# Moving the second half of a 32x32-tiled recurrence off the array's diagonal, with its residual masked by VectorE

## What is computed

```python
k = rope(x @ Wk.T); v = x @ Wv.T          # (B, H, S, 32), B = 4, H = 16
def step(W, kv):                          # W starts as the identity, 32 x 32 for each of 64 (batch, head)
    kc, vc = kv                           # 16 tokens
    z = einsum('bhsd,bhde->bhse', kc, W)
    grad = einsum('bhsd,bhse->bhde', kc, (z - vc) * inv_n)
    return (W - LR * grad, z)
_, zs = lax.scan(step, W0, (k_c, v_c))    # 32 steps
out = layernorm(zs) * ln_gamma + ln_beta; attn = out @ Wo.T
x = layernorm(x + attn)
```

## Time and profile before

| | us |
|---|---|
| median of 3 runs (lowest, highest) | 699.45 (698.92, 700.35) |
| the profiled execution's own time | 699.14 |
| its span in the profile | 697.3 |
| PE busy in the span | 677.9 (97%) |
| DVE busy | 443.7 (64%) |
| ACT busy | 315.0 (45%) |
| POOL busy | 305.8 (44%) |

### The profile page before, as it was taken

How to read it: one execution, slowest core, us unless ns; L and a number is a source line. 1 busy time by engine, 2 the same in 40 slices (tenths; PEclk the granted TensorE clock), 3 DMA queues, 4 the chain that set the end, 5 groups by cost and what they waited for, 6 DMA issues and landing times.

```text
span 697.3 us, 16575 instructions
## 1 busy us (share of the span) xinstructions
PE 677.9 (97%) x6884; PEld 547.4 (78%) x6884; DVE 443.7 (64%) x772; ACT 315.0 (45%) x599; POOL 305.8 (44%) x342
## 2 busy tenths in 40 slices
PE   9999999999999999999999999999999999999994
PEld 7767777777877778787888788888887888888883
DVE  4998676778856455378875554645466357666565
ACT  5653544545645532341123465655576452141232
POOL 2657667767636532011004345434552235626232
PEclk9999999999999999999999999999999999999998
DMA  8221242331341424000062577677547765414222
GB/s 277 87 65 46 66 141 66 93 111 52 110 154 64 141 61 156 31 14 1 1 241 78 195 273 256 208 273 259 179 161 253 260 204 182 121 60 123 74 76 90
DMA packets 65710, 92.47 MB, mean 133 GB/s; under 512 B 16672, under 2 KB 31776, under 8 KB 65632
## 3 DMA queue, kind: packets, MB, share of 16 engines
q1 hardware_dynamic: 59952, 72.76, 30.9%
q0 software_dynamic: 5680, 18.62, 9.2%
HBM read 67.56 MB, written 23.79 MB: 131 GB/s over the span
## 4 chain that ended last, share of the span: by engine, by line
PE 65%; DVE 17%; issue 5%; POOL 5%; ACT 4%; DMA 2%; DVEq 0%; POOLq 0%; ACTq 0%
PE bank L1255 13%; PE bank L1168 10%; PE bank L1061 10%; PE bank L1292 7%; PE bank L1115 6%; PE bank L1181 4%; PE bank L1094 4%; PE bank L1081 3%; DVE x L1465 3%; PE bank L1242 2%; DMA xg<-yd,SI 2%; DVE x L1513 2%; PE bank L1268 2%; POOL xg L1832 2%; DVE sg L1455 2%
## 5 line engine op out<-in xcount | busy, mean ns | idle before, releaser
L1794 POOL TENSOR_TENSOR xl<-RAW,xh 128x1024 fp32r<-128x1024 f32 x23 | 55.4, 2409 | 124.9 <-ACT xh L1655 124.8
L1168 PE MATMUL bank<-XH,GH 128*128 128x512 f32 x256 | 101.7, 397 | 0.5 <-ACT sg L1669 0.3
L1671 ACT ACTIVATE ah<-sg 128x512 fp32r<-128x512 f32 x48 | 30.3, 632 | 158.0 <-DVE sg L1455 158.0
L1168 PE MATMUL bank<-XH,GL 128*128 128x512 f32 x256 | 99.8, 390 | 0.0
L1168 PE MATMUL bank<-XL,GH 128*128 128x512 f32 x256 | 99.7, 390 | 0.0
L1455 DVE TENSOR_TENSOR sg<-sg,bank 128x512 f32<-128x512 f32 x48 | 32.9, 685 | 78.5 <-PE bank L1255 42.3
L1807 POOL DMA_INDIRECT xg<-x1d,idxu x39 | 42.3, 1085 | 69.9 <-DVE idxu L880 41.2
L1445 DVE TENSOR_TENSOR GL<-RAW,GH 128x1024 fp32r<-128x1024 f32 x42 | 50.3, 1224 | 11.0 <-ACT GH L1650 8.5
L1168 PEld LDWEIGHTS bank<-XH,GH 128*128 128x128 f32 x256 | 48.1, 188 | 11.3 <-ACT sg L1669 0.7
L1457 DVE TENSOR_TENSOR al<-sg,ah 128x512 fp32r<-128x512 f32 x48 | 35.2, 734 | 33.5 <-ACT ah L1671 32.8
L1168 PEld LDWEIGHTS bank<-XH,GL 128*128 128x128 f32 x256 | 48.1, 188 | 10.3
(11 more groups left out here) (254 smaller groups left out, 1608.9 us busy)
## 6 DMA issues: line engine op xcount, KB each, us to landing
RAW<-in_wgu SPq DMA_DIRECT2D x13, 1024.0 KB
yd<-RAW SPq DMA_DIRECT2D x39, 256.0 KB
RAW<-in_wsgu SPq DMA_DIRECT2D x14, 512.0 KB
RAW<-in_wd SPq DMA_DIRECT2D x13, 512.0 KB, 5.5
x<-in_xtok SPq DMA_DIRECT2D x16, 256.0 KB, 3.0
x1d<-x SPq DMA_DIRECT2D x16, 256.0 KB, 2.5
RAW<-in_wsd SPq DMA_DIRECT2D x8, 512.0 KB, 4.0
out_x<-x SPq DMA_DIRECT2D x16, 256.0 KB, 2.0
```

The lines of the kernel that those rows point to most:

```text
L1168: t = e.matmul(bank[b][:], (GL if wl else GH)[:, w % 2, k, c:c + 128], (XL if xlo else XH)[q % 2][:, k, :], start=(k == 0 and not wl and n ...
L1794: e.tensor_tensor(DL[:, w % 2, :, :], draw[:, raw_of(w), :, :], DH[:, w % 2, :, :].bitcast(F32), ALU.subtract).then_inc(*mark("low p", "d" ...
```

## The change

The second half (h = 1) moves to tiles off the diagonal: in z it takes rows g and columns (g + 64) % 128, in g rows (g + 64) % 128 and columns g. Its residual, values and rows of z thereby lie 64 partitions away from where they were, and so the host swaps the matching rows of Wv, Wo, gamma and beta. Within a block the two halves now alternate: four matmuls of half 0, four of half 1, for each `pp`. A block waits for both halves' operands before it begins.

The mask of half 1 goes from ScalarE to VectorE: one TENSOR_TENSOR with the mask behind the two subtractions (`rmask v`), where ScalarE had two ACTIVATEs. The mask of half 0 stays. The key turn for u >= 4 becomes two STREAM_TRANSPOSEs of 64 partitions that cross over, where there was one of 128.

```diff
                     for pp in range(4):
-                        hg, bp = 2 * h + pp // 2, pp % 2
-                        c = hg * 512 + (n % 8) * 64 + bp * 32
-                        for g in range(0, 128, 32):
-                            t = e.matmul(bank[h][g:g + 32, pp * 64:pp * 64 + 64], KK[g:g + 32, par, 0, c:c + 32], W[h][g:g + 32, pp * 64:pp * 64 + 64],
-                                         start=True, stop=True)
-                    t.then_inc(*mark("z", n, h))
+                        for h in (0, 1):
+                            c = (2 * h + pp // 2) * 512 + (n % 8) * 64 + pp % 2 * 32
+                            for g in range(0, 128, 32):
+                                o = (g + 64 * h) % 128
+                                t = e.matmul(bank[h][o:o + 32, pp * 64:pp * 64 + 64], KK[g:g + 32, par, 0, c:c + 32], W[h][g:g + 32, pp * 64:pp * 64 + 64],
+                                             start=True, stop=True)
+                            if pp == 3:
+                                t.then_inc(*mark("z", n, h))
                 elif step == "g":
-                    n, h = a
+                    n, = a
                     q, par = n // 8, n // 8 % 2
-                    e.wait_ge(*on("rmask", n, h))
+                    e.wait_ge(*on("rmask", n))
+                    e.wait_ge(*on("rmask v", n))
...
+                                t = e.matmul(bank[2 + h][g:g + 32, pp * 64:pp * 64 + 64], KK[o:o + 32, par, 1, c:c + 32],
+                                             r[o:o + 32, n // 2 % 2, n % 2, 256 * h + pp * 64:256 * h + pp * 64 + 64],
+                                             start=False, stop=(n == 31), skip_group_check=True)
...
+        def turn_keys(e, q, u):
+
+            if u < 4:
+                e.transpose(key_cols(q, u), key_rows(q, u)).then_inc(*mark("kturn", q, u))
+            else:
+                e.transpose(key_cols(q, u)[64:128], key_rows(q, u)[0:64])
+                e.transpose(key_cols(q, u)[0:64], key_rows(q, u)[64:128]).then_inc(*mark("kturn", q, u))
...
+                    if h == 1:
+                        r4 = r[:, n // 2 % 2, n % 2, 256:512].rearrange("p (a x) -> p a x", a=4)
+                        e.wait_ge(*on("rsub", n, 1))
+                        e.tensor_tensor(r4, r4, mask[:].unsqueeze(1).to_broadcast([128, 4, 64]), ALU.mult).then_inc(*mark("rmask v", n))
...
+    left = np.concatenate([np.arange(256), np.arange(256, 512).reshape(2, 2, 64)[:, ::-1].reshape(-1)])
```

More of the change, by code:

```diff
@@ L1071, in tensor @@
                 elif step == "z":
-                    n, h = a
+                    n, = a
                     q, par = n // 8, n // 8 % 2
-                    e.wait_ge(*on("wcopy", n - 1, h))
+                    for h in (0, 1):
+                        e.wait_ge(*on("wcopy", n - 1, h))
                     if n % 8 == 0:
@@ L1090, in tensor @@
                     for pp in range(4):
-                        hg, bp = 2 * h + pp // 2, pp % 2
-                        c = hg * 512 + (n % 8) * 64 + bp * 32
-                        for g in range(0, 128, 32):
-                            t = e.matmul(bank[2 + h][g:g + 32, pp * 64:pp * 64 + 64], KK[g:g + 32, par, 1, c:c + 32],
-                                         r[g:g + 32, n // 2 % 2, n % 2, 256 * h + pp * 64:256 * h + pp * 64 + 64],
-                                         start=False, stop=(n == 31), skip_group_check=True)
-                    t.then_inc(*mark("g", n, h))
+                        for h in (0, 1):
+                            c = (2 * h + pp // 2) * 512 + (n % 8) * 64 + pp % 2 * 32
+                            for g in range(0, 128, 32):
+                                o = (g + 64 * h) % 128
+                                t = e.matmul(bank[2 + h][g:g + 32, pp * 64:pp * 64 + 64], KK[o:o + 32, par, 1, c:c + 32],
+                                             r[o:o + 32, n // 2 % 2, n % 2, 256 * h + pp * 64:256 * h + pp * 64 + 64],
+                                             start=False, stop=(n == 31), skip_group_check=True)
+                            if pp == 3:
+                                t.then_inc(*mark("g", n, h))
                 elif step == "wo bias":
@@ L1575, in scalar @@
                     n, h = a
-                    e.wait_ge(*on("rsub", n, h))
-                    r4 = residues(n, h)
-                    e.activation(r4[:, :, 0, :], r4[:, :, 0, :], ACT.Copy, scale=mask[:, 0:1])
-                    e.activation(r4[:, :, 1, :], r4[:, :, 1, :], ACT.Copy, scale=mask[:, 32:33]).then_inc(*mark("rmask", n, h))
+                    if h == 0:
+                        r4 = residues(n, 0)
+                        e.wait_ge(*on("rsub", n, 0))
+                        e.activation(r4[:, :, 0, :], r4[:, :, 0, :], ACT.Copy, scale=mask[:, 0:1])
+                        e.activation(r4[:, :, 1, :], r4[:, :, 1, :], ACT.Copy, scale=mask[:, 32:33]).then_inc(*mark("rmask", n))
                 elif step == "g":
-                    n, h = a
-                    if n < 31:
+                    n, = a
+                    for h in (0, 1) if n < 31 else ():
                         e.wait_ge(*on("g", n, h))
@@ L1757, in gpsimd @@
                     i, = a
-                    e.wait_ge(*on("rmask", 2 * i + 1, 1))
+                    e.wait_ge(*on("rmask", 2 * i + 1))
+                    e.wait_ge(*on("rmask v", 2 * i + 1))
                     for m in range(2):
```

26 lines of the change are left out of this document (13 added, 13 removed).

## The result

| | before | after |
|---|---|---|
| median of the runs, us | 699.56 (698.92 to 700.35, 4 runs) | 709.83 (708.02 to 710.78, 4 runs) |
| profiled execution, us | 699.14 (span 697.3) | 710.78 (span 709.0) |
| mean granted clock | 0.996 (profiled execution) | 0.984 to 0.989 (the runs) |

The changed kernel takes 1.0149 times as long as the one before, with an interval of 1.0137 to 1.0161. It is slower by 10.3 us, where some 14 us less had been forecast, and lies outside the forecast's range.

A forecast was written before the change was run, and what follows sets the result against it. TensorE was taken as the bound from 58.36 to 196.84 us, VectorE's chain before: 699.14 - 28.8 + 2.9 + 3.6 + 3.6 + 0.4 + 2.0 + 2.0 = 684.8, as a median 685.1 us. Range: 674 to 697.

The forecast's parts named there:

- What bounds the kernel: Whole run: TensorE the bound from 58.36 to 196.84 us, VectorE's chain in the first four steps, GpSimd also in the last quarter.
- The block: Each z and g block: 16 clusters become 8, saving 0.45 us a block, 28.8 us for 64 blocks.
- the issue can bring four more into that gap: Inside a block: four more matmuls start in the at least 0.03 us free of starts in each cluster.
- VectorE's additions: VectorE in the recurrence: 32 masks at 0.55 us and eight more turns at 0.65, in all 22.8 us.
- The chain from z to g: Between z and g: g can start 2.3 us behind z; steps 13, 19, 22 lose about 0.15 each, 0.4 us.
- The start: From 28.82 to 58.36 us: first wo comes 2.9 us later, and eight blocks' saving of 3.6 is not had.
- The quarter ends: Steps 7 to 8 and the second quarter's end: VectorE's mask and turn delay g, 1.8 us each, 3.6 in all.
- The tight part: From 154.80 to 187.57 us: VectorE's idle 5.8 us against 8.55 wanted, 2.0 us lost.
- The last quarter: From 196.84 to 260 us: the chain through GpSimd and transfers becomes no shorter; between 0 and 5, taken as 2.0 us lost.
- From 260 us to the end: The stretch after 260 us: nothing changes, it stays at 437 us.
- Tiles of one row group take turns: Rival on the blocks: they stay at 1.02 us and only costs remain; 707 us, range 702 to 711, chance 0.16.
- VectorE becomes the bound everywhere: Rival: masks at 0.75 us and 12% of VectorE's time lost to waits; 694 us, 690 to 698, chance 0.14.

The follow-up runs named there:

- the kernel with the mask put back: Changed kernel with the mask of half 1 back on ScalarE, all else as changed: 701.5 us, ratio 1.0032 to the kernel before.
- the kernel with the halves in turn: Kernel before with z and g alternating halves under joined waits; tiles on the diagonal, masks on ScalarE, keys turned in one piece: 705.9 us, ratio 1.0100.
- holding TensorE busy: Changed kernel with ten unread 128x128 matmuls ahead of each of two TensorE waits, first g and first wo: 705.7 us, ratio 1.0094.
- that with the pause: Changed kernel with two unread 128x128 matmuls between the first and last 32 records of every z and g block: 730.9 us in its one execution.
- six steps apart and TensorE kept busy: Kernel with six steps apart plus unread matmuls, two ahead of the first g's wait and six ahead of the first wo's: 697.0 us, ratio 0.9964.
- six steps apart: Changed kernel with both masks on ScalarE and halves one after the other, with own waits, at n = 1, 7, 15, 19, 22, 25: 697.9 us, ratio 0.9986.
- the kernel with both halves on the diagonal: Changed kernel with both halves on diagonal tiles and key turns in one piece; alternation, joined waits and VectorE's mask stay: 711.5 us, ratio 1.0165.

## Why the prediction was wrong, step by step

- **What bounds the kernel**: right as read. VectorE sets the first four steps, TensorE steps 4 to 23. What was not read from it is how thin that bound is: with blocks only 0.24 us shorter, chains through VectorE set the length of the odd steps.
- **The block** (-28.8 us): the term was mis-sized. Its mechanism held (eight streams in the time of four, 16 to 20 matmuls in flight), and so did the step "the issue can bring four more into that gap", but for 32 records only. For the second 32 it failed; a block takes 0.78 us and not 0.57, a saving of 0.24 and not 0.45. 64 blocks would be 15.4 us; on the steps it is 0.4 to 0.5 us each where nothing else waits. The earlier trace rows could not show it: at four records in 0.06 us nothing ran short to the end of the block. The sum had no term for the rate at which records can follow one another over a whole block; it was taken as free because a gap was seen.
- **VectorE's additions** (22.8 us): right. 32 masks of 0.547 (forecast 0.55) and eight more turns of 0.70 (0.65 forecast) are 23.1 us. The page's 24.9 holds something else besides: the 15 `ol`, which nobody changed, went from 15.6 to 20.0 us (mean 1.04 to 1.33), and the subtractions from 26.2 to 24.0. `ol` took 19.0 in the kernel with the mask put back as well, so its price follows the order of work around it, not the mask alone; the prediction had no term for that. (GpSimd's share, which it leaned on, is 62 to 71% of the first three quarters in the earlier trace rows, not 65 to 75.) ScalarE lost 20.7 us and not 25, since its mask operations overlap in time (before, 122.20 for 0.41, then 122.52). A turn of 64 partitions costs as much as one of 128 (0.706 against 0.712), the upper of the two ends.
- **The chain from z to g** (+0.4): the time was right, 2.38 us behind z at step 13 where 2.3 was forecast. The step that failed is what it was compared with. I asked only when g could start, and not who else waits on VectorE behind the mask. It is `ol`, and behind it `wo` and the next z: step 13 takes 6.99 us, where 6.58 less two blocks would be 5.7 by the forecast. The instructions queued behind the added one had to be listed, and TensorE waits for one of them.
- **The start** (+2.9, and 3.6 not had): forecast was the first `wo` at 58.3; it came at 61.78, and z(4) at 66.29. Its parts on VectorE were right (mask 0.69 to 0.42, turns 0.7 each). Missing were the joined waits (0.9 us at step 1 in the kernel with the halves in turn) and the clock: two idle times of 2.6 us, opened by these delays, each followed by work at half speed; holding TensorE busy gave 3.4 us back by z(4). The prediction gave the clock no term at all. By its terms the first four steps were to take 32.4 us; they took 36.9.
- **The quarter ends** (+3.6): g of step 8 at 97.31, 10.15 us behind step 7's subtraction at 87.16, forecast 10.2. Right in size, and step 7 is 0.95 us longer than before as that implies. But the cause named (VectorE's extra mask and turn) is only a part: the turns cost nothing there, the mask 0.60 in the kernel before, and the joined waits alone 0.86.
- **The tight part** (+2.0): 35.25 us between z(18) and z(23) where 32.77 had been, so 2.5 longer, and the saving of ten blocks was not had either. Steps 18 and 19 are the worst (8.48 and 7.42 against 6.60 and 6.58), and there TensorE idles again (2.3 us of 166 to 171), waiting with z of step 19 for ScalarE's copies into `WA` and `WB`. The prediction weighed only VectorE's idle time here. The chain of waits goes through three engines: from GpSimd's work on the residual through the mix and L1360 on VectorE to ScalarE, where the copies stand behind `kS`:

```profile
165.86 0.58 POOL rstd L1803
...
168.13 0.69 DVE RAW L1360
...
168.90 0.10 ACT kS L1579
...
169.39 0.38 ACT WA L1604
```

The clock falls behind that idle time:

```profile
166.00:171.00 5.00, 2.68 (x100) 1.92 (x85) 4.55 (x12) 2.10 (x5) 4.20 (x6) 1.00 0.03 8
171.00:176.00 5.00, 5.00 (x79) 3.63 (x77) 4.93 (x6) 1.62 (x5) 4.92 (x5) 0.66 0.36 108
```

- **The last quarter** (+2.0): steps 24 to 30 came out 0.3 us shorter in all. Step 30 alone is 1.4 us longer (8.81 against 7.38), in the stretch from 263 to 268 us where the clock is at 0.66.
- **From 260 us to the end**, "unchanged": 1.9 us longer. From z(31) to the end the profiles (that with the pause left aside) have 440.6 to 443.8 us, and this follows none of the parts: the longest is that with only the mask put back, the shortest that with six steps apart and TensorE kept busy. For the longest the record has a part of the reason: TensorE is idle there for 2.0 us up to 681.85, where the kernel before is idle for 0.45, and the clock is at 0.66 from 683 to 688. For the others it stays open.
- **The rivals.** "Tiles of one row group take turns" has the measured time inside its range (702 to 711) by luck: it is refuted in its mechanism. "VectorE becomes the bound everywhere" is nearest in mechanism, and was priced 16 us too low, because its losses were set against 28.8 us of saving.

Summed up by the medians: joining the halves costs 6.7 us (699.2 to 705.9), shifting the tiles, with the turns it needs, gives 4.4 back (to 701.5), moving the mask costs 8.3 (to 709.8). These prices hold in this order of the parts; the mask alone on the kernel before costs 7.0. And each has the clock's falls in it that came with the part. With the turns at the 3.3 us they cost by themselves, the costs are 18.3 us where 10.9 had been forecast, and the gain is 7.7 where 25.2 (28.8 less the 3.6 not had) had been. So some 17 us of the difference between forecast and result are saving that was not had, and some 7 are costs that had no term or too small a one.

## What to carry to other kernels

A gap between starts shows that something else paces them, not that twice as many could follow one another for a whole burst: look how the same engine behaves over a burst twice as dense, or insert a pause and see whether the speed returns. Joining two halves of a step to save issue time also joins their waits, and the pipeline through three engines that two separate halves had is lost; do it only at those steps where other work lies between. Before adding an instruction to a queue, name what stands behind it and who waits for that, and where it opens an idle time of TensorE like those of 1.2 to 2.6 us here, add the slower clock behind it to the price.

## What the runs showed of the hardware

- Small matmuls on eight tiles of 32x32, two in one row group, run at full rate together: eight records of 64 columns in 0.056 us. After 32 records in a row the rate falls to one in 12 ns on average, and two larger matmuls between, which put 0.79 us between the two halves' records, restore it.
- The granted clock fell to its lower level behind idle times of 2.6 us in the changed kernel, and it fell (to a mean of 0.78 over 36 to 41 us) behind idle times of 0.8, 0.3 and 1.2 us in that with six steps apart. In that with the mask put back the last of these was 0.7 us, and it did not fall. Equal idle times did not always end alike: in the kernel with both halves on the diagonal and in the kernel before with the mask on VectorE, TensorE was idle for 0.7, 0.3 and 0.85 us up to 34.4 us, and the clock from 33 to 38 us was 0.66 in the one and 1.00 in the other.
- Over the ten executions of one kernel the time went with the mean clock, 704.3 us at 0.984 and 697.2 at 0.995. That is some 0.6 us for each 0.001, and a spread of 1% where the kernel before has 0.2 to 0.3%. That equal idle times end in a fallen clock in some executions and not in others would explain it; only one execution of each kernel is profiled, so within one kernel this is not shown, and between kernels it is (the point above, and the idle times of 1.72 us in the last two kernels).
- `ol`, an operation of VectorE with two operands in SBUF, took a mean of 1.33 us and up to 1.77. In step 13 it ran from 130.00 to 131.75 while GpSimd's addition of the same kind ran from 129.74 to 131.20. The Trainium skill, "SBUF — State Buffer", section "Who interferes with whom", says that such a pair shares one pair of ports and that one waits for the whole of the other. By that `ol` had to wait until 131.20 here: 131.75 less 131.20 is 0.55 us, not far from the 0.68 of its shortest instance in this kernel, so the trace agrees roughly.
